# Two heads on the partitions: attention scores from two fp16 parts in a macaron block

## The chip, the cores and the metric

The kernel runs on one core of one Trainium2 chip. The metric is the device time of one execution in microseconds (us); the comparison is the median of several runs of the kernel before and of the changed one.

## What is computed

A "macaron" block over x of shape (1, 4096, 256), all in fp32: a mixture-of-experts layer with weight one half, an attention layer, and the same mixture again. Each works on a layer-normalised x and adds to x.

```python
x = x + 0.5 * ffn(layernorm(x), Wg, W1, W2, W3, Ws1, Ws2, Ws3)
x = x + attn(layernorm(x), qkv_w, qkv_b, proj_w, proj_b)
x = x + 0.5 * ffn(layernorm(x), Wg, W1, W2, W3, Ws1, Ws2, Ws3)

def attn(x, qkv_w, qkv_b, proj_w, proj_b):      # 16 heads of 16 columns
    q, k, v = split_heads(x @ qkv_w.T + qkv_b)   # each (16, 4096, 16)
    scores = q @ k.T / 4                         # (16, 4096, 4096)
    out = softmax(scores) @ v
    return merge_heads(out) @ proj_w.T + proj_b
```

The ffn routes each token to 4 of 32 experts and adds a shared expert; the change leaves it alone, but for one helper that it shares.

## The kernel before

The attention layer is written in five pieces, one after another, with a barrier of all engines between them (`attention`, L724).

**project_heads (L747)** computes the layer norm of x, Q, K and V. The weights are transposed on TensorE (PE), ScalarE (ACT) copies them out. VectorE (DVE) takes the statistics of all 32 tiles of 128 tokens in `normalise_stats`. Then a loop goes over 8 blocks of 512 tokens: DVE normalises four tiles, PE turns them, ACT copies them; PE multiplies V (L837) and DVE adds its bias into `V` in SBUF (L919); PE multiplies four tensors of 128 columns, two of Q and two of K (L854). Each of the four is split into three bf16 parts whose sum is the fp32 value: ACT writes the first part (L892) and the full value (L894) from PSUM, DVE the rest, the second and the third part (L937, L939, L941), and SP stores the three to `part_d` in DRAM (L789) out of two part buffers. ACT squares the full value (L900), PE sums the squares of each head (L846), for a bound on the scores.

**bound_shift (L951)** makes from the norms a shift for each query, so that no exponential overflows (softmax does not change with it), and a flag that says whether the bound is tight enough. **exact_shift (L1021)** runs only where the flag says no.

**attend (L1096)** is the main part. A scores matmul gives 128 keys x 512 queries. Six products of the parts (0·0, 0·1, 0·2, 1·0, 1·1, 2·0) are stacked on the partitions, 6 x 16 rows, with three rows more for the shift, 99 rows. `Q` and `K` of two heads lie in `RA` (index r); SP loads them from `part_d`, 13 transfers a head (L1144). One step k stands for 128 keys and 2048 queries of a head:
- PE: two times two scores matmuls into `psS`, three slots of 1024 columns (L1188);
- ACT: two exponentials of 128x1024 from `psS` to `probs`, a ring of four buffers (L1233);
- PE: four "weighing" matmuls (L1202), each `values` (V of the head beside ones, 32 columns) against 512 columns of `probs`, into four strips of 32 partitions of `psO`; fp32 operands run as two passes, so the trace has eight records. The ones give the sum of the probabilities.

After 32 steps (4096 keys) DVE copies `psO` out (L1255) and takes the reciprocal (L1257), and SP stores both to `head_d` (L1161). The order on each engine is written out by hand in `body`; a body holds two heads, 128 steps, and `rounds` loops it seven times and writes out the eighth. PE issues, for each k, the first half of the scores of step k+2, the weighing of step k, the second half of step k+2:

```python
def body(r2, last):
    for k in range(STEPS):
        ahead(r2, (k + 2) * CH, last)
        weigh(r2, k)
        ahead(r2, (k + 2) * CH + 1, last)
```

The semaphores: `scored` counts chunks of scores, `exped` exponentials, `pv` weighings. Scores wait for the exponential that frees their slot, a weighing for the exponentials of its step, and the first exponential of a step for the weighing two steps before (L1232).

**project_out (L1264)** multiplies by the reciprocals and the output weights, and adds to x.

## Time and profile before

| | |
|---|---|
| median of 3 runs | 3764.67 us (3762.79 to 3764.81) |
| span of the profiled execution | 3764.7 us; no other time is shown for it, and a run of 3764.67 is among the three |
| mean granted TensorE clock | 0.929 of full speed |
| PE busy (matmuls) | 3159.2 us, 84% |
| ACT busy | 2390.9 us, 64% |
| DVE busy | 921.9 us, 24% |
| POOL busy | 750.2 us, 20% |
| head projections and shift bound | 722 to 945.3 us |
| attention loops | 945.3 to 3009 us |
| output projection | 3009 to 3068 us |

How to read it: the span runs from the first to the last instruction of one profiled execution. "Busy" is time in which at least one instruction of the engine runs; matmuls are pipelined, each lasting longer than its slot, so that a PE that is always busy need not work at its peak. PE stands for matmuls and PEld for the loads of their weights. The granted clock is the share of full speed that the throttle gives TensorE. Rows name line, engine, operation, output and inputs by the program's names.

### The profile page before, as it was taken

Reading aid. Unit: us, or ns where it says so; the run is one execution under the profiler, and the core shown is the slowest. Engines: PE = TensorE matmul, PEld = TensorE weight load, DVE = VectorE, ACT = ScalarE, POOL = GpSimd, SP = SyncE. Lnnn points to the kernel's source line nnn. Section 1 sums busy time; section 2 is a strip of 40 time slices with the busy share of each in tenths; the row PEclk is TensorE's granted clock in tenths of the full one; section 3 lists DMA queues with packets and bytes.
Section 4 is the critical chain, followed back from the end, with each engine's and each line's share of the span. In section 5 each row is a group of like instructions: output and inputs, shape, how many; then the busy total and the mean of one; then the engine's idle time right before and its main releaser. Section 6 shows DMA issues by size and latency. Waiting matters only on the chain. (4 is left out here: it accounts for less than half of the span.)

```text
span 3764.7 us, 60460 instructions
## 1 busy us (share of the span) xinstructions
PE 3159.2 (84%) x16839; PEld 1226.4 (33%) x16840; DVE 921.9 (24%) x2298; ACT 2390.9 (64%) x3265; POOL 750.2 (20%) x1131
## 2 busy tenths in 40 slices
PE   4379985474999999999999999999999954799863
PEld 4156653242222222222222222222222252466532
DVE  3843334555000000000000000000000057433253
ACT  1034420043999999999999999999999900244300
POOL 0455547400000000000000000000000023555465
PEclk9999998686999999999999999999999965899987
DMA  5134443322111011011101110110110050244534
GB/s 166 58 105 131 128 111 95 120 84 69 23 21 24 4 24 21 4 24 21 23 4 24 21 22 6 24 21 4 24 21 6 4 170 13 84 132 128 121 89 123
DMA packets 143809, 216.15 MB, mean 57 GB/s; under 512 B 24992, under 2 KB 109728, under 8 KB 140448
## 3 DMA queue, kind: packets, MB, share of 16 engines
q1 hardware_dynamic: 103472, 121.24, 12.7%
q0 software_dynamic: 27648, 75.53, 7.8%
q10 hardware_dynamic: 12496, 16.78, 1.5%
q8 instruction: 124, 2.03, 0.2%
q14 instruction: 69, 0.57, 0.1%
HBM read 133.37 MB, written 80.08 MB: 57 GB/s over the span
## 5 line engine op out<-in xcount | busy, mean ns | idle before, releaser
L1233 ACT ACTIVATE probs<-psS 128x1024 f32<-128x1024 f32 x2048 | 1983.8, 1021 | 59.9 <-PE psO L1202 32.5
L1188 PE MATMUL psS<-RA 99*128 99x512 bf16 x4096 | 1072.7, 384 | 51.2 <-DMA RA<-part_d 19.1
L1202 PE MATMUL psO<-probs,values 128*32 128x512 f32 x8192 | 1097.6, 608 | 0.4 <-ACT probs L1233 0.4
L1188 PEld LDWEIGHTS psS<-RA 99*128 99x128 bf16 x4096 | 317.1, 98 | 1163.5 <-ACT probs L1233 870.3
L1255 DVE COPY sums<-psO 128x512 f32<-128x512 f32 x32 | 22.1, 692 | 1943.4 <-PE psO L1202 1943.4
L1295 POOL TENSOR_TENSOR RA<-RA,pbias 128x1024 f32<-128x1024 f32 x8 | 21.5, 2702 | 2092.2 <-DMA RA<-x_d 2092.2
L538 POOL DMA_INDIRECT xg<-xn_d,index x320 | 313.1, 978 | 264.6 <-PE psX L554 152.9
L562 PE MATMUL psH<-WE,xgt 128*128 x1280 | 355.9, 401 | 0.0
L1202 PEld LDWEIGHTS psO<-probs,values 128*32 128x32 f32 x8192 | 161.6, 108 | 439.9 <-issue 426.3
L609 ACT ACTIVATE gate<-psH 128x128 f32<-128x128 f32 x320 | 88.8, 278 | 326.2 <-PE psH L562 326.2
L669 POOL DMA_INDIRECT Y<-pair_d,cindex x256 | 246.3, 962 | 120.0 <-issue 70.5
L562 PEld LDWEIGHTS psH<-WE,xgt 128*128 128x128 f32 x1280 | 220.1, 192 | 42.6 <-issue 2.5
L577 PE MATMUL psO<-WE,hidt 128*128 x640 | 213.8, 416 | 0.2
L702 ACT ACTIVATE sgate<-psA 128x512 f32<-128x512 f32 x32 | 19.1, 597 | 306.7 <-PE psB L683 306.7
L692 PE MATMUL psZ<-ws,shid 128*128 128x256 f32 x256 | 95.4, 539 | 128.9 <-DVE shid L709 110.4
L554 PE MATMUL psX<-ident,xg 128*128 128x128 f32 x640 | 135.3, 294 | 66.9 <-DMA xg<-xn_d,index 64.3
L589 DVE COPY xgt<-psX 128x256 f32<-128x256 f32 x320 | 135.9, 425 | 148.1 <-PE psX L554 143.1
L618 ACT ACTIVATE ob<-psO 128x256 f32<-128x256 f32 x320 | 122.9, 384 | 65.7 <-PE psO L577 60.2
L594 DVE TENSOR_TENSOR hid<-gate,psH 128x128 f32<-128x128 f32 x320 | 92.1, 288 | 282.3 <-ACT gate L609 282.3
L719 DVE SCALAR_TENSOR_TENSOR RA<-Y,pair_weight,RA 128x256 f32 x256 | 124.3, 485 | 124.3 <-DMA Y<-pair_d,cindex 105.6
L609 ACT ACT_TABLE_LOAD x2 | 2.6, 1283 | 204.7 <-PEq L284 204.7
L554 PEld LDWEIGHTS psX<-ident,xg 128*128 128x128 f32 x640 | 73.1, 142 | 151.4 <-DMA xg<-xn_d,index 105.3
(191 smaller groups left out, 1980.7 us busy)
## 6 DMA issues: line engine op xcount, KB each, us to landing
pair_d<-ob SPq DMA_DIRECT2D x320, 128.0 KB, 1.8
RA<-part_d SPq DMA_DIRECT2D x192, 128.0 KB
part_d<-parts SPq DMA_DIRECT2D x32, 384.0 KB, 3.2
xn_d<-xn SPq DMA_DIRECT2D x64, 128.0 KB, 1.7
hd<-head_d SPq DMA_DIRECT2D x16, 512.0 KB, 6.7
xg<-xn_d,index POOLq DMA_INDIRECT x320, 2.8
RA<-in_x SPq DMA_DIRECT2D x8, 512.0 KB, 7.4
WE<-in_W ACTq DMA_DIRECT2D x1, 4096.0 KB, 22.9
```

Of the source, the lines that this page charges most:

```text
L538: pool.indirect_dma_start(xg[:, u, :], None, xn_d, bass.IndirectOffsetOnAxis(ap=index[:, u:u + 1], axis=0))\
L554: last = pe.transpose(psX[s % 2][:, c * P:(c + 1) * P], xg[:, (s + 2) % U, c * P:(c + 1) * P], ident[:, :])
L562: last = pe.matmul(psH[(s + 1) % 2][:, :], xgt[:, (s + 1) % 2, c * P:(c + 1) * P], WE[:, e, c * 2 * H:(c + 1) * 2 * H], start=(c == 0), st ...
L577: pe.matmul(psO[(s - 1) % 2][:, :], hidt[:, (s - 1) % 2, :], WE[:, e, DC * 2 * H:], start=True, stop=True).then_inc(sem("down"), 1)
L589: v.tensor_copy(xgt[:, s % 2, :], psX[s % 2][:, :]).then_inc(sem("xgt_ready"), 1)
L618: act.activation(ob[:, (s - 1) % U, :], psO[(s - 1) % 2][:, :], ACT.Copy).then_inc(sem("ob_ready"), 1)
L669: pool.indirect_dma_start(Y[:, s, :], None, pair_d, bass.IndirectOffsetOnAxis(ap=index[:, w, u, k:k + 1], axis=0))\
L692: last = pe.matmul(psZ[u % 2][:, :], hid[:, m, u * P:(u + 1) * P], ws2[:, m, :], start=(m == 0), stop=(m == HSC - 1))
L719: v.scalar_tensor_tensor(X[:, t, :], Y[:, (u % 2) * TOPK + k, :], pair_weight[:, bass.ds(t, 1), k], X[:, t, :], ALU.mult, ALU.add).then_in ...
L1188: last = pe.matmul(psS[slots[m]][:, b * BLK:(b + 1) * BLK], K[r][0:QROWS, kt * P:(kt + 1) * P], Q[r][0:QROWS, at:at + BLK], start=True, st ...
L1202: last = pe.matmul(psO[q % 2][32 * j:32 * (j + 1), :], values[:, r, kt, :], probs[:, m % PS, at:at + BLK], start=(kt == 0), stop=(kt == KT ...
L1233: act.activation(probs[:, m % PS, :], psS[slots[m]][:, :], ACT.Exp, scale=SCALE).then_inc(sem("exped"), 1)
```

## The change

The parts and the shapes change, from the weights on:

- **Two fp16 parts.** fp16 holds more digits than bf16 but a smaller range. `balance_weights` therefore scales the rows of the query weights and biases by powers of two and those of the keys by the inverse, before the weights are turned; it stands on DVE between the two halves of the statistics (`normalise_stats` now has two loops of four rounds, in the other layers too). ACT writes the high part, DVE the low part in one operation from PSUM. There are four part buffers, one for each of the four tensors of a block. PE waits for the split in place of ACT's second identity.
- **Two heads on the partitions.** Three products (0·0, 1·0, 0·1) take 3 x 16 rows, with three rows for the shift 51. The even head of a pair lies at partition 0, the odd one at 64. A unit is one scores matmul; successive units alternate between the heads.
- **Wider exponentials.** 128 keys x 4 units make a step. Scores go in chunks of three units (1536 columns), two slots of `psS`; 128 units of a group make 42 chunks of three and one of two. ACT does one exponential per chunk, into a ring of four buffers of 1536 columns. A body holds two pairs of heads: 8 groups, 344 chunks, 256 steps; `rounds` loops it three times and writes out the fourth.
- **Shift bound.** Two reductions over 4096 columns and the zeroing of `shift_d` go from DVE; POOL writes the ones and the step (1024) beside the keys in this piece, in eight memsets, and SP loads the operands of the first two pairs here.

```diff
-NPART = 3
-KROWS = 6 * HD
-QROWS = KROWS + NPART
+NPART = 2
+NSHIFT = 3
+SHIFT_ROW = 2 * HD
+LAST_ROW = SHIFT_ROW + NSHIFT
+ROWS = LAST_ROW + HD
+STEP0 = 1024.0
+HALF_ROWS = P // 2
...
+    for half in range(2):
+        with v.Fori(0, NT // 8) as i:
+            for u in range(4):
+                t = i * 4 + (half * (NT // 2) + u)
+                v.bn_stats(stats[:, bass.ds(t, 1), :], X[:, t, :]).then_inc(act_sem, 1)
+        if half == 0 and between is not None:
+            between()
...
+def balance_weights(v, link, raw, bias, square_sum, span, expo_i, expo_f, power, scaled):
+    HB = 2 * D // P // 2
+    link(v.tensor_tensor(span[:, :], bias[:, :], bias[:, :], ALU.mult))
+    link(v.scalar_tensor_tensor(span[:, :], square_sum[:, :], float(D), span[:, :], ALU.mult, ALU.add))
+    link(v.tensor_scalar(expo_i[:, :], span[:, :].bitcast(I32), 23, None, ALU.arith_shift_right))
+    link(v.tensor_copy(expo_f[:, :], expo_i[:, :]))
+    link(v.tensor_tensor(expo_f[:, 0:HB], expo_f[:, HB:], expo_f[:, 0:HB], ALU.subtract))
+    link(v.tensor_copy(expo_i[:, 0:HB], expo_f[:, 0:HB]))
+    link(v.tensor_scalar(expo_i[:, 0:HB], expo_i[:, 0:HB], 2, None, ALU.arith_shift_right))
+    link(v.tensor_copy(expo_f[:, 0:HB], expo_i[:, 0:HB]))
+    link(v.tensor_scalar(expo_f[:, 0:HB], expo_f[:, 0:HB], 60.0, -60.0, ALU.min, ALU.max))
+    link(v.tensor_scalar(power[:, 0:HB], expo_f[:, 0:HB], 2.0 ** 23, 127.0 * 2 ** 23, ALU.mult, ALU.add))
+    link(v.tensor_scalar(power[:, HB:], expo_f[:, 0:HB], -2.0 ** 23, 127.0 * 2 ** 23, ALU.mult, ALU.add))
+    link(v.tensor_tensor(bias[:, :], bias[:, :], power[:, :].bitcast(F32), ALU.mult))
+    for b in range(2 * HB):
+        v.tensor_scalar(raw[:, b, :], raw[:, b, :], power[:, b:b + 1].bitcast(F32), None, ALU.mult).then_inc(scaled, 1)
...
+                for n, b in enumerate((6, 7, 4, 5, 0, 1, 2, 3)):
+                    if b < NE:
+                        pe.wait_ge(sem("w_scaled"), b + 1)
+                    if n >= 2:
+                        pe.wait_ge(sem("w_out"), n - 1)
...
-                                pe.wait_ge(sem("q_out"), j * NE + (e - 1))
+                                pe.wait_ge(sem("split"), j * NE + (e - 1))
...
-                            act.wait_ge(sem(f"part_stored{e % 2}"), (j * (NE // 2) + e // 2) * 16 + 16)
-                            act.activation(parts[:, e % 2, 0, :], psQ[e % 2][:, :], ACT.Identity, bias=bias[:, e:e + 1])
+                            act.wait_ge(sem(f"part_stored{e}"), j * 16 + 16)
                             total = key_sum[:, e - 2, bass.ds(j, 1)] if e >= 2 else None
-                            act.activation(full[:, e % 2, :], psQ[e % 2][:, :], ACT.Identity, bias=bias[:, e:e + 1],
-                                           accum_out=total)\
-                               .then_inc(sem("q_out"), 1)
-                            act.wait_ge(sem("q_out"), j * NE + (e + 1))
-                            if e == 0:
-                                act.wait_ge(sem("measured"), j + 1)
-                            act.activation(square[:, e, :], full[:, e % 2, :], ACT.Square).then_inc(sem("squared"), 1)
+                            act.activation(parts[:, e, 0, :], psQ[e % 2][:, :], ACT.Identity, bias=bias[:, e:e + 1],
+                                           accum_out=total).then_inc(sem("high"), 1)
+                            if e >= 1:
+                                squared(j, e - 1)
+                            if e == NE - 1:
+                                squared(j, e)
...
+                def balance():
+                    v.wait_ge(sem("bias"), 16)
+                    v.wait_ge(sem("w_squared"), NE)
+                    balance_weights(v, own.link, raw, bias, square_sum, span, expo_i, expo_f, power, sem("w_scaled"))
+                normalise_stats(v, own.link, X, stats, mean, rstd, tmp, var, sem("stats"), sem("sqrt"), balance)
+                v.wait_ge(sem("vbias"), 16)
...
-                            n = j * NE + e
-                            f, r, g = full[:, e % 2, :], rest[:, :], parts[:, e % 2, :, :]
-                            v.wait_ge(sem("q_out"), n + 1)
-                            if not (isinstance(n, int) and n == 0):
-                                v.wait_ge(sem("split"), n)
-                            v.tensor_tensor(r, f, g[:, 0, :], ALU.subtract).then_inc(sem("rest"), 1)
-                            v.wait_ge(sem("rest"), n + 1)
-                            v.tensor_copy(g[:, 1, :], r).then_inc(sem("mid"), 1)
-                            v.wait_ge(sem("mid"), n + 1)
-                            v.tensor_tensor(g[:, 2, :], r, g[:, 1, :], ALU.subtract).then_inc(sem("split"), 1)
+                            v.wait_ge(sem("high"), j * NE + (e + 1))
+                            v.scalar_tensor_tensor(parts[:, e, 1, :], psQ[e % 2][:, :], bias[:, e:e + 1], parts[:, e, 0, :],
+                                                   ALU.add, ALU.subtract).then_inc(sem("split"), 1)
...
+            @block.gpsimd
+            def _(pool):
+                for r in range(2):
+                    for base in (0, HALF_ROWS):
+                        at = base + SHIFT_ROW
+                        pool.memset(K[r][at:at + NSHIFT, :], 1.0).then_inc(sem("ones"), 1)
+                        pool.wait_ge(sem("ones"), 4 * r + base // 32 + 1)
+                        pool.memset(K[r][at:at + 1, :], STEP0).then_inc(sem("ones"), 1)
+                        pool.wait_ge(sem("ones"), 4 * r + base // 32 + 2)
             @block.sync
             def _(sp):
-                sp.wait_ge(sem("zeroed"), 1)
-                for n in range(1, NPART):
-                    sp.dma_start(shift_d[n], zero[:, :]).then_inc(sem("shift_out"), 16)
+                for r in range(2):
+                    load_parts(sp, Q[r], K[r], part_d, r, sem(f"ops{r}"))
                 sp.wait_ge(sem("negated"), 1)
-                sp.dma_start(shift_d[0], shift[:, :]).then_inc(sem("shift_out"), 16)
-                sp.wait_ge(sem("shift_out"), 16 * NPART)
-def query_rows(sp, dst, part_d, h, signal):
-    row = 0
-    for part, times in ((0, 3), (1, 2), (2, 1)):
-        for _ in range(times):
-            sp.dma_start(dst[row:row + HD, :], part_d[part, bass.ds(h * HD, HD), :]).then_inc(signal, 16)
-            row += HD
-def key_rows(sp, dst, part_d, h, signal):
-    for n, part in enumerate((0, 1, 2, 0, 1, 0)):
-        sp.dma_start(dst[n * HD:(n + 1) * HD, :], part_d[part, bass.ds(h * HD + D, HD), :]).then_inc(signal, 16)
-def exact_shift(nc, sem, sb, pb, RA, ident, safe, part_d, shift_d):
-    ops = RA[:, :].bitcast(BF16).rearrange("p (n t) -> p n t", n=4)
+                sp.dma_start(shift_d[1], shift[:, :]).then_inc(sem("shift_out"), 16)
...
+def head_parts(sp, dst, base, part_d, first, order, signal):
+    for row, part in zip((0, HD, LAST_ROW), order):
+        sp.dma_start(dst[base + row:base + row + HD, :], part_d[part, bass.ds(first, HD), :]).then_inc(signal, 16)
+def load_parts(sp, Qr, Kr, part_d, pair, signal):
+    for n in range(2):
+        h = pair * 2 + n
+        head_parts(sp, Qr, n * HALF_ROWS, part_d, h * HD, (0, 1, 0), signal)
+        head_parts(sp, Kr, n * HALF_ROWS, part_d, h * HD + D, (0, 0, 1), signal)
+def load_shift(sp, Qr, shift_d, pair, signal):
+    for n in range(2):
+        at = n * HALF_ROWS + SHIFT_ROW
+        sp.dma_start(Qr[at:at + NSHIFT, :], shift_d[:, bass.ds(pair * 2 + n, 1), :].rearrange("a h t -> (a h) t"))\
+          .then_inc(signal, 16)
...
-    QU = T // (4 * BLK)
-    W = 2 * BLK
-    CH = 4 * BLK // W
-    STEPS = 2 * QU * KT
-    SLOTS, PS = 3, 4
...
+    QG = 4
+    GU = 4 * KT
+    WIDE = 3
+    PAIRS = NH // 2
+    RING = 4
+    GROUP = [WIDE] * (GU // WIDE) + ([GU % WIDE] if GU % WIDE else [])
+    UNITS = 2 * QG * GU
+    first, chunk_of = [], []
+    for g in range(2 * QG):
+        for size in GROUP:
+            first.append(len(chunk_of))
+            chunk_of += [len(first) - 1] * size
+    CHUNKS = len(first)
+    STEPS = UNITS // 4
+    HALF_CHUNKS = CHUNKS // 2
+    first.append(UNITS)
     CREDIT = 4
-    n_chunks = STEPS * CH
-    slots = [n % SLOTS for n in range(n_chunks)]
-    slots[-4:] = [0, 1, 2, 1]
-    LOADS = 13
-    def since(n):
-        d = 1
-        while slots[(n - d) % n_chunks] != slots[n]:
-            d += 1
-        return d
+    LOADS = 14
...
+                            sp.wait_ge(sem("scored"), r2 * CHUNKS + HALF_CHUNKS * (r + 1))
                             carried(sp, sem("seen_sp"))
-                            load(h + 2, r)
+                            load_parts(sp, Q[r], K[r], part_d, r2 * 2 + (2 + r), sem(f"ops{r}"))
...
+                def scores(r2, m, waits):
+                    if m % HALF_CHUNKS == 0:
+                        pe.wait_ge(sem(f"ops{m // HALF_CHUNKS}"), r2 * (16 * LOADS) + 16 * LOADS)
+                    if waits:
+                        pe.wait_ge(sem("exped"), r2 * CHUNKS + (m - 1))
+                    for u in range(first[m], first[m + 1]):
+                        r, q, kt, j = u // (QG * GU), u // GU % QG, u // 4 % KT, u % 4
+                        rows = slice(j % 2 * HALF_ROWS, j % 2 * HALF_ROWS + ROWS)
+                        at = (2 * q + j // 2) * BLK
+                        last = pe.matmul(psS[m % 2][:, (u - first[m]) * BLK:(u - first[m] + 1) * BLK],
+                                         K[r][rows, kt * P:(kt + 1) * P], Q[r][rows, at:at + BLK], start=True, stop=True)
...
+                        m, at = place(4 * k + j)
+                        last = pe.matmul(psO[q % 2][32 * j:32 * (j + 1), :], values[:, r, j % 2, kt, :],
+                                         probs[:, m % RING, at:at + BLK], start=(kt == 0), stop=(kt == KT - 1))
...
+                    k = 0
+                    for m in range(0, CHUNKS, 2):
+                        ahead(r2, m + 2, last)
+                        while k < STEPS and place(4 * k + 3)[0] <= m:
+                            weigh(r2, k)
+                            k += 1
+                        ahead(r2, m + 3, last)
+                    for k in range(k, STEPS):
                         weigh(r2, k)
...
-                        if m % CH == 0:
-                            act.wait_ge(sem("pv"), r2 * STEPS + (m // CH + 1))
-                        act.activation(probs[:, m % PS, :], psS[slots[m]][:, :], ACT.Exp, scale=SCALE).then_inc(sem("exped"), 1)
+                    for m in range(CHUNKS):
+                        act.wait_ge(sem("scored"), r2 * CHUNKS + (m + 1))
+                        before = m - RING
+                        done = final_step(before) + 1 if before >= 0 else final_step(CHUNKS + before) + 1 - STEPS
+                        act.wait_ge(sem("pv"), r2 * STEPS + (done + CREDIT))
+                        n = (first[m + 1] - first[m]) * BLK
+                        act.activation(probs[:, m % RING, 0:n], psS[m % 2][:, 0:n], ACT.Exp, scale=SCALE).then_inc(sem("exped"), 1)
```

**The order on PE in the loops.** L1188 and L1202 are scores and weighing before, L1256 and L1276 after; the rows named REGISTER_ALU make the value of a wait. First two steps in steady state before:

```order
L1185 REGISTER_ALU
L1188 MATMUL psS<-RA 128x512 x2
L1185 REGISTER_ALU
L1188 MATMUL psS<-RA 128x512 x2
L1202 MATMUL psO<-probs,values 32x512 x4
L1185 REGISTER_ALU
L1188 MATMUL psS<-RA 128x512 x2
```

The same place after the change, four chunks (three steps):

```order
L1276 MATMUL psO<-probs,values 32x512 x8
L1251 REGISTER_ALU
L1256 MATMUL psS<-RA 128x512 x3
L1251 REGISTER_ALU
L1256 MATMUL psS<-RA 128x512 x3
L1276 MATMUL psO<-probs,values 32x512 x4
L1251 REGISTER_ALU
L1256 MATMUL psS<-RA 128x512 x3
L1251 REGISTER_ALU
L1256 MATMUL psS<-RA 128x512 x3
L1276 MATMUL psO<-probs,values 32x512 x8
```

A weighing stood behind every four scores matmuls; now one or two of them, in turns, stand behind six, with a wait ahead of each three.

**The order on POOL ahead of the loops.** `RA` holds the operands, `values` the values and their ones. Before, in the loops' own piece:

```order
L1136 MEMSET values 128x32x16
L1138 MEMSET RA 3x4096
L1136 MEMSET values 128x32x16
L1138 MEMSET RA 3x4096
```

After, the first eight in `bound_shift`, the last in `attend`:

```order
L1048 MEMSET RA 3x4096
L1050 MEMSET RA 1x4096
L1048 MEMSET RA 3x4096
L1050 MEMSET RA 1x4096
L1048 MEMSET RA 3x4096
L1050 MEMSET RA 1x4096
L1048 MEMSET RA 3x4096
L1050 MEMSET RA 1x4096
L1015 UNCONDITIONAL_BRANCH
L1209 UNCONDITIONAL_BRANCH
L1213 MEMSET values 128x32x16 x4
```

Two memsets of 4096 columns have become eight, and they stand a piece earlier.

## Rows read from the trace of the kernel before

**Rows 1.** Windows: span part, then us, PE, PEld, DVE, ACT, POOL busy, granted clock, DMA, GB/s
```profile
722.00:945.30 223.30, 127.41 (x372) 70.17 (x373) 121.62 (x235) 77.08 (x140) 8.95 (x7) 0.74 0.32 91
...
945.30:3009.00 2063.70, 2031.17 (x12288) 478.70 (x12288) 129.33 (x76) 1992.76 (x2055) 0.00 (x0) 0.99 0.10 17
...
954.83:1200.50 245.67, 245.57 (x1500) 58.22 (x1498) 12.42 (x7) 242.25 (x250) 0.00 (x0) 1.00 0.06 11
```

**Rows 2.** Timeline, one steady step: start us, us, engine, line, operation, count
```profile
955.66 1.06 PE L1202 MATMUL psO<-probs,values 128*32 128x512 f32 x8
...
955.75 1.02 ACT L1233 ACTIVATE probs<-psS 128x1024 f32<-128x1024 f32 x1
...
956.11 0.61 PE L1202 MATMUL psO<-probs,values 128*32 128x512 f32 x4
...
956.66 0.39 PE L1188 MATMUL psS<-RA 99*128 99x512 bf16 x1
...
956.66 1.04 PE L1188 MATMUL psS<-RA 99*128 99x512 bf16 x4
...
956.79 1.03 ACT L1233 ACTIVATE probs<-psS 128x1024 f32<-128x1024 f32 x1
...
957.63 1.06 PE L1202 MATMUL psO<-probs,values 128*32 128x512 f32 x8
```

**Rows 3.** Timeline of the loops: the first step, and two later rounds' first exponentials
```profile
947.73 3.77 ACT L1233 ACTIVATE probs<-psS 128x1024 f32<-128x1024 f32 x4
...
948.80 0.13 PEld L1188 LDWEIGHTS psS<-RA 99*128 99x128 bf16 x2 [1.68 <-ACT probs L1233]
...
1203.44 3.77 ACT L1233 ACTIVATE probs<-psS 128x1024 f32<-128x1024 f32 x4
...
1462.22 3.77 ACT L1233 ACTIVATE probs<-psS 128x1024 f32<-128x1024 f32 x4
```

**Rows 4.** Groups by line: count, busy us, mean ns, idle before and releasers
```profile
L1233 ACT ACTIVATE probs<-psS 128x1024 f32<-128x1024 f32 x2048 | 1983.8, 1021 | 59.9 <-PE psO L1202 32.5
...
L609 ACT ACTIVATE gate<-psH 128x128 f32<-128x128 f32 x320 | 88.8, 278 | 326.2 <-PE psH L562 326.2
...
L941 DVE TENSOR_TENSOR parts<-rest,parts 128x512 bf16<-128x512 f32 x32 | 22.2, 692 | 1.1
...
L1138 POOL MEMSET RA<- 3x4096 bf16 x2 | 7.2, 3588 | 0.1
```

**Rows 5.** Timeline of two blocks of the head projections
```profile
832.62 0.69 ACT L892 ACTIVATE parts<-psQ,bias 128x512 bf16<-128x512 f32 x1 [8.93 <-PE psQ L854]
...
839.29 0.69 ACT L892 ACTIVATE parts<-psQ,bias 128x512 bf16<-128x512 f32 x1 [1.87 <-DMA part_d<-parts]
...
844.93 3.78 PE L837 MATMUL psV<-wt,axnt 128*128 128x256 f32 x8 [4.69 <-DVE RB L919]
...
852.59 0.69 ACT L892 ACTIVATE parts<-psQ,bias 128x512 bf16<-128x512 f32 x1 [9.33 <-PE psQ L854]
```

**Rows 6.** Timeline of the start of the head projections
```profile
725.69 10.32 SPq L781 DMA_DIRECT2D bias<-in_qkv_b  x1
...
725.99 9.95 DVE L189 BATCH_NORM_STATS2 astats<-RA  x28 [0.36 <-issue]
...
742.32 1.38 DVE L924 TENSOR_SCALAR axn<-RA,amean,arstd 128x256 f32<-128x256 f32 x4 [3.62 <-DMA vbias<-in_qkv_b]
...
746.00 6.45 PE L837 MATMUL psV<-wt,axnt 128*128 128x256 f32 x16 [1.24 <-ACT axnt L883]
```

**Rows 7.** Timeline of the shift bound and the first scores
```profile
908.01 0.14 DVE L948 COPY key_mean<-psN 16x1 f32<-16x1 f32 x1 [0.29 <-PE psN L865]
...
909.65 1.76 DVE L971 MEMSET zero_shift<- 16x2048 uint32 x1 [1.49 <-PEq L775]
...
930.79 2.73 SPq L1012 DMA_DIRECT2D RA<-part_d  x6
...
945.29 2.74 PE L1188 MATMUL psS<-RA 99*128 99x512 bf16 x6 [19.05 <-DMA RA<-part_d]
```

270 lines of the change are left out of this document (136 added, 134 removed).

## The prediction

> **What bounds the kernel now.** I read the windows first. Of 3764.7 us, 2063.7 go to the attention loops and 223.3 to the head projections and the shift bound ahead of them [rows 1]; both feed-forward layers lie outside the change, but for one helper. In the loops PE is busy 98%, ACT 97%, so neither share says who waits. The timeline of one steady step does. PE starts the second pass of a weighing (fp32, four strips) at 956.11, four scores matmuls at 956.66 and the next weighing at 957.63, with no hole beyond about 0.1 us at each switch: the 0.55 from 956.11 to 956.66 is 0.43 of streaming plus 0.12, and four scores at 0.22 each (1.04 less the last one's 0.39, by three) leave 0.09 of the 0.97 [rows 2]. On ACT the exponential at 956.79 starts 1.04 after that at 955.75, though an exponential that waits for nothing follows its forerunner by 0.92 (four take 3.77: 3.77 less 1.02, by three) [rows 2, 3]. It starts 1.13 after the weighing at 955.66 began, each time: it waits for the ring of probabilities. So **PE sets the pace**, one step of 4 x 512 columns in 1.965 us (250 exponentials, two a step, in 245.67 [rows 1]), and ACT has 0.12 us a step to spare.
>
> **Loops, part 1: what each instruction costs after.** An activation of 128 columns takes 278 ns and one of 1024 takes 1021 [rows 4]: 0.83 ns a column and 0.17 us fixed. Of 1536 columns one takes 1.45; waiting for nothing it follows its forerunner by 0.92 + 0.43 = 1.35. The weighings keep form and number (0.45 + 0.43, and the switch). The scores shrink from 99 rows to 51. That alone I cost at nothing: a matmul's time is that of its 512 columns. But two heads now lie at rows 0 and 64, and successive matmuls alternate. The trace has no row-packed pair. The nearest row is the weighing: four matmuls on disjoint column strips, in two passes, take 1.06 together against 0.61 for one pass [rows 2]. Bounds for the pair: 0.22 (together) and 0.44 (one after the other). I take 0.22, because the strips that exist do overlap. Three scores matmuls then take two slots, 0.43, instead of 0.65. The Trainium skill (TensorE: Matmul & The Clock Gate, Part 3: Packing small matmuls) gives 3.07 times for four row tiles, not 4; were a pair as inefficient, my estimate by that page is 0.28 for it, and the sum below would be 15 us higher. No row here can show that.
>
> **Loops, part 2: the order, which is what counts.** The rows of the order show it: after the scores of chunk m+2 (they wait for exponential m) come one or two weighings, then the scores of m+3. With four part buffers of probabilities, exponential m+2 may start only when chunk m-2 has been weighed out, and in every second group that is the first weighing *behind* the scores of m+2. So there is a cycle from exponential m to m+2:
> - exponential m starts; scores that wait for its end start 1.07 later at 1024 columns (947.73 to 948.80 [rows 3]), so 1.07 + 0.43 = 1.50 at 1536;
> - three scores until the weighing begins: 0.97 less two of the four slots of 0.22 = 0.54;
> - weighing begins until the exponential that waits for it: 955.66 to 956.79 = 1.13 [rows 2].
>
> Together 3.17 for two chunks, where ACT alone would need 2 x 1.35 = 2.70. A group is 128 units: 42 chunks of three and one of two, 43 in all, so groups start alternately on even and odd chunks. Even start: 21 pairs x 3.17 and 0.6 for the short one, partly under the last hole: 67.2. Odd start: the cycle binds only in every second pair (for the other the weighing is already done). A binding pair costs 3.17, the other 2.70, and 0.08 more where scores stand behind two weighings: 5.95 for four chunks, 63.5 a group. Eight of each: 8 x 67.2 + 8 x 63.5 = **1046 for half the heads, 2091 in all**, against 2048 exponentials x 0.983 = 2012.5 now: **+79**.
>
> **Loops, part 3: turn-arounds.** The loop body comes round in 258.8 us (1203.44 to 1462.22 [rows 3]), of which 256 x 0.983 = 251.6 are the pace: 7.2 here, and 7.6 on the mean of five such rounds: table load, cold PE, "issue". Six such ends now (eight rounds, the last written out), two afterwards (four rounds, bodies of 344 exponentials): **-30**. An operand load of a later pair starts when its scores are issued, a half body (250 us) ahead; its 14 transfers are covered.
>
> **Head projections.** A block of 512 tokens takes 19.97 (832.62 to 852.59 [rows 5]); 19.9 on the mean of the eight between 746.00 and 908.01 [rows 6, 7], with 2.8 of tail. In it PE needs at full clock, by the slots of rows 2: V 16 x 0.22 = 3.5, queries and keys 16 x 0.44 = 7.0, turning about 1.0, norms 4 x 0.22 = 0.9: 12.4. The rest is waiting: ACT's first identity waits 1.87 for a store out of the two part buffers; PE waits 4.69 for V's additions, which stand behind DVE's three splitting operations, and then takes 3.78 for eight V matmuls, which are 8 x 0.22 at full clock [rows 5]. After: four part buffers, no second identity on ACT, one DVE operation for three (0.69, as L941 [rows 4]; were it a fused one's double, V's additions still come within a slot), and a third reduction of norms under PE. PE now releases a psQ buffer only at the split; that falls under the next tensor. I take 13.3 a block (12.4 and about 0.9 for switches and the loops' branches): 8 x 6.6 = **-53**; bounds 16 a block (-31) and 12.6 (-58).
>
> **Before them.** The weights' balancing stands on DVE between the halves of the statistics and waits for the bias. That load now precedes the copy of x; its issue alone takes 10.32 from 725.69 [rows 6], and a landing of some 2.5 gives 738. Then 12 chained small ones (0.2 each) and four of about 0.4: 742; half of the statistics (9.95 for 28 of 32 [rows 6]: 5.7) and the moments (2.5): xn at 751 against 742.32 [rows 6]: **+9**, bounds +4 and +12. The helper's second loop costs the two other layers about 1 us each: **+2**.
>
> **Shift bound and start.** DVE loses two reductions of 4.4 and a memset, but POOL gains eight memsets one behind another in the same block, where the nearest row has 3588 ns for 3 x 4096 [rows 4]: 28.6 (a block begins 1.6 after 908.01, at 909.65). From there to the first load of operands, 930.79, are 21.1 [rows 7]; DVE's last result comes 4.2 ahead of that, barriers and the check of the flag, and these stay. The loads of the first two pairs go under the memsets; behind the barrier only the shift rows are left, two issues of 0.3 and a landing of about 3, where now 14.5 pass from 930.79 to 945.29 [rows 7]. So 1.6 + 28.6 + 4.2 + 3.7 = 38.1 after 908.01, against 37.3: **+1**. If one row costs a third of three, -9.
>
> **Sum.** +79 - 30 - 53 + 9 + 2 + 1 = +8. The profiled execution has 3764.7 us of span and no time around it that is shown; the median of the runs is 3764.67, so the sum starts from either. That gives 3773; taking back 2 for slots rounded up (0.215 as 0.22), I state **3771**. Differences under 0.2% (7.5 us) no measurement here tells from none.
>
> **Rivals.**
> 1. *The row pair does not overlap* (slower; the change would not do what the stacking says). For it: in the trace all scores matmuls follow each other at 0.22, and no row-packed pair exists. Against: column strips overlap. Price: 0.22 more in each cycle, 3.39 for a pair, and in odd groups 0.22 more at the scores behind two weighings too (5.95 + 2 x 0.22 = 6.39 for four chunks): 21 x 3.39 + 0.6 = 71.8 and 68.1, eight of each 1119, 2238 in all, +147; less 3 for the short ones: **3915**. It decides early: 252 binding pairs, so a row pair that takes 0.25 in place of 0.22 costs 8 already. Chance 0.13. The Trainium skill (TensorEngine Tiling, PSUM pressure) says that row tiles may not write one PSUM bank together; here each unit has its own bank, so this is no reason for it.
> 2. *The ring does not bind* (faster): the first weighing is out before ACT asks. For it: ACT's wait of 0.12 today is small, and the order of the wait is read from instructions, not seen for this shape. Then only scores behind two weighings delay ACT: ready 1.50 + 0.54 + 2 x 0.90 + 0.10 + 0.60 = 4.54 after exponential m, where ACT wants them after 3 x 1.35 = 4.05. Four chunks take 5.9: 344 x 5.9 less 32 x 0.43 = 2016, -75: **3696**. Were ACT alone the bound, 1344 x 1.35 + 32 x 0.92 = 1844 would give 3524 (-247), but a pair of weighings (1.8) and two switches do not fit under one exponential. Chance 0.12, the latter 0.02 of it.
> 3. *The clock falls* (slower): PE would stand still about a quarter of each cycle, where it is granted 1.00 now [rows 1]; in the projections at 57% busy it was 0.74. At 1.2 GHz streaming takes twice the time, as V's eight matmuls show (3.78 for 1.76 [rows 5]): the cycle's 0.54 and the weighing's 0.90 double, 1.4 more in 3.17, and 2091 x 0.44 = +920: near 4690. Against: no hole would be over 0.6 us. Chance 0.05.
>
> **How the numbers follow.** The forecast's case has 0.70. Its terms move by 21 (the cycle, 1% of 2091), 22 (blocks) and 5 (start), seldom together: 3735 to 3810. Of it 0.28 lies below 3757, 0.26 within 0.2%, 0.46 above 3772. Faster: 0.20 + 0.12 = 0.32; same 0.18; slower 0.32 + 0.13 + 0.05 = 0.50. For 8 in 10 the range must take in the non-overlapping pair at 3915, and below the forecast's own low end part of the way to rival 2: 3715 to 3920.
>
> **What would show it.** Right: exponentials 1.45 long, their starts in turns 1.35, 1.82 / 1.42, 1.74; ACT waiting for psO; pairs of scores matmuls starting within 0.01; blocks of 13 us; memsets of 28 us under the first loads; two turn-arounds. Wrong: ACT without holes (rival 2), scores at 0.22 each (rival 1), a clock under 1.00 in the loops (rival 3). The weakest step is the cycle: if starts two chunks apart differ by 2.9 or less, this forecast fails.

## The result, and the profile after

| | before | changed |
|---|---|---|
| median | 3764.74 us (3762.79 to 3765.47, 4 runs) | 6375.73 us (6375.38 to 6376.65, 4 runs) |
| ratio | 1 | 1.6935 (95% interval 1.6911 to 1.6959) |
| span of the profiled execution | 3764.7 | 6374.0 |
| mean granted clock | 0.929 | 0.758 |

The prediction said 3771, with a range of 3715 to 3920. It was wrong by 2605 us. The page of the changed kernel shows where they lie: the rows of section 2 (each digit a fortieth of the span, 159 us) and the costliest groups.

```profile
span 6374.0 us, 74864 instructions
...
PE   3797667777777777777777888888888888865984
...
DVE  5433558888888888888889000000000000036334
ACT  1241210000000000000000999999899988931420
...
PEclk9998765555555555555555999999999999976997
...
L1147 DVE TENSOR_REDUCE half_max<-psSx 128x2048 f32 x1024 | 2297.6, 2285 | 275.9 <-PE psSx L1127 242.6
L1127 PE MATMUL psSx<-exact_ops 51*128 51x512 f16 x4096 | 1913.8, 620 | 666.2 <-DVE half_max L1147 417.0
L1305 ACT ACTIVATE probs<-psS 128x1536 f32<-128x1536 f32 (+1 forms) x1376 | 1913.8, 1441 | 188.7 <-PE psO L1276 184.5
L1256 PE MATMUL psS<-RA 51*128 51x512 f16 x4096 | 824.2, 385 | 360.5 <-ACT probs L1305 351.7
```

From the seventh slice to the twenty-second ACT does nothing, DVE is busy and the granted clock is 0.5. The two groups at the head, L1147 and L1127, are in `exact_shift`, which reads every score once (1024 maxima over 2048 columns, 2.28 us each) to find the shift of each query. The trace of before has no such group: there the branch was not taken. The timeline of the changed kernel gives the piece its borders:

```profile
854.06 0.15 DVE L1000 COPY key_mean<-psN 16x1 f32<-16x1 f32 x1 [0.29 <-PE psN L910]
...
863.37 0.14 DVE L1029 TENSOR_SCALAR safe<-worst 1x1 int32<-1x1 f32 x1
...
899.05 1.46 PE L1127 MATMUL psSx<-exact_ops 51*128 51x512 f16 x3 [35.92 <-DMA exact_ops<-part_d]
...
1198.01 9.10 DVE L1147 TENSOR_REDUCE half_max<-psSx 128x2048 f32 x4 [0.17 <-PE psSx L1127]
...
3502.50 1.46 PE L1256 MATMUL psS<-RA 51*128 51x512 f16 x6 [6.53 <-POOL values L1213]
```

The flag is written at 863.37, and the first scores of the loops start at 3502.50, 2648 after `key_mean`, where [rows 7] has 37.3. Outside that stretch the kernel's time is near what was forecast. The windows (columns as in [rows 1]) show three stretches: the head projections and the bound up to the end of the memsets, the exact pass, and the loops. Behind them stands the steady state of the loops.

```profile
721.80:884.10 162.30, 109.07 (x371) 61.25 (x371) 82.22 (x190) 58.45 (x117) 30.01 (x12) 0.82 0.41 107
884.10:3502.50 2618.40, 1920.18 (x4112) 434.99 (x4113) 2327.16 (x1126) 0.00 (x0) 2.75 (x4) 0.50 0.03 5
3502.50:5614.00 2111.50, 1757.13 (x12288) 347.94 (x12288) 129.17 (x75) 1917.60 (x1379) 0.00 (x0) 0.99 0.05 9
```

```profile
3519.17 2.89 ACT L1305 ACTIVATE probs<-psS 128x1536 f32<-128x1536 f32 x2 [0.38 <-PE psO L1276]
3522.34 2.79 ACT L1305 ACTIVATE probs<-psS 128x1536 f32<-128x1536 f32 x2 [0.28 <-PE psO L1276]
3525.51 2.89 ACT L1305 ACTIVATE probs<-psS 128x1536 f32<-128x1536 f32 x2 [0.38 <-PE psO L1276]
...
3575.59 5.58 ACT L1305 ACTIVATE probs<-psS 128x1536 f32<-128x1536 f32 x4 [0.38 <-PE psO L1276]
3581.54 5.58 ACT L1305 ACTIVATE probs<-psS 128x1536 f32<-128x1536 f32 x4 [0.38 <-PE psO L1276]
```

Two exponentials every 3.17 us in a group that starts on an even chunk, four every 5.95 in one that starts on an odd chunk, each time behind a hole that `psO` (the weighing) ends. These are the two numbers of the forecast's cycle.

### The profile page after: what moved, and what is told of

Its sections match the earlier page's. It is cut to its first block and busy times, and to the rows that moved or that the text cites. A ratio compares the mean times of both kernels' runs of the same rounds, so it can differ in the third digit from the quotient of the medians.

```text
span 6374.0 us, 74864 instructions
## 1 busy us (share of the span) xinstructions
PE 4789.0 (75%) x20949; PEld 1523.3 (24%) x20952; DVE 3209.2 (50%) x3378; ACT 2297.0 (36%) x2566; POOL 774.0 (12%) x1140
## 5 line engine op out<-in xcount | busy, mean ns | idle before, releaser
L1147 DVE TENSOR_REDUCE half_max<-psSx 128x2048 f32 x1024 | 2297.6, 2285 | 275.9 <-PE psSx L1127 242.6
L1127 PE MATMUL psSx<-exact_ops 51*128 51x512 f16 x4096 | 1913.8, 620 | 666.2 <-DVE half_max L1147 417.0
L1305 ACT ACTIVATE probs<-psS 128x1536 f32<-128x1536 f32 (+1 forms) x1376 | 1913.8, 1441 | 188.7 <-PE psO L1276 184.5
L1256 PE MATMUL psS<-RA 51*128 51x512 f16 x4096 | 824.2, 385 | 360.5 <-ACT probs L1305 351.7
L1276 PE MATMUL psO<-probs,values 128*32 128x512 f32 x8192 | 1025.9, 603 | 0.5 <-ACT probs L1305 0.5
L1127 PEld LDWEIGHTS psSx<-exact_ops 51*128 x4096 | 433.3, 125 | 2136.7 <-issue 2136.7
L1256 PEld LDWEIGHTS psS<-RA 51*128 51x128 f16 x4096 | 151.8, 93 | 1275.3 <-ACT probs L1305 983.4
L1276 PEld LDWEIGHTS psO<-probs,values 128*32 128x32 f32 x8192 | 196.2, 109 | 494.2 <-issue 484.0
```

The lines of the kernel that those rows point to most:

```text
L1127: last = pe.matmul(psS[n][:, b * BLK:(b + 1) * BLK], ops[0:ROWS, 0, bass.ds(t * P, P)], ops[0:ROWS, 1, n * HALF + b * BLK:n * HALF + (b + ...
L1147: v.tensor_reduce(half[:, bass.ds(t, 1), n], psS[n][:, :], AX, ALU.max).then_inc(sem("x_read"), 1)
L1256: last = pe.matmul(psS[m % 2][:, (u - first[m]) * BLK:(u - first[m] + 1) * BLK], K[r][rows, kt * P:(kt + 1) * P], Q[r][rows, at:at + BLK], ...
L1276: last = pe.matmul(psO[q % 2][32 * j:32 * (j + 1), :], values[:, r, j % 2, kt, :], probs[:, m % RING, at:at + BLK], start=(kt == 0), stop= ...
L1305: act.activation(probs[:, m % RING, 0:n], psS[m % 2][:, 0:n], ACT.Exp, scale=SCALE).then_inc(sem("exped"), 1)
```

## The experiments

The chips that these runs were on differ in time by 0.7%, so each was timed beside the kernel before on its own chip, and runs of different chips are compared by their ratios to it.

### The branch: rounding, and the limit of the flag

Why should the flag fall, when the scores are the same? `balance_weights` takes for each of 256 pairs of rows (a query's and its key's) the difference of two exponents, shifts it right by two and scales one side up and the other down. An arithmetic shift rounds towards minus infinity: 0 to 3 give 0, but -1 gives -1. By a working of mine from the inputs (not read from a run), 67 of the 256 differences are -1 and none is beyond 1; their queries are halved, their keys doubled. Products stay the same, but the bound multiplies the norm of the longest query of a head by that of its longest key (and of its mean key), and the doubled rows of one then meet the rows of the other that weren't halved: 284.5 by that working, against 167.4 without scaling, and the flag allows 280 (SAFE, which is 70, divided by the scale of a quarter). Theory A: the rounding sets off the branch, and without it the forecast stands.

`e1_round` adds 2 before the shift, so that the quarter is rounded to the nearest (-1 to 0):

```diff
-    link(v.tensor_copy(expo_i[:, 0:HB], expo_f[:, 0:HB]))
+    link(v.tensor_scalar(expo_i[:, 0:HB], expo_f[:, 0:HB], 2.0, None, ALU.add))
```

> Edit: in the balancing of the weights 2 is added before the exponent difference is shifted right by two, so that a difference of -1 gives 0 as +1 does, not -1; nothing else. Theory A (the floor of the shift moves a factor of two from some query rows to key rows, that blows up the bound on the scores, and the flag sends the kernel into exact_shift): the branch is gone, 3502.5 us (first scores in the changed kernel) less 892 (854.06 + 0.6 + 29.4 of memsets + 4.2 + 3.5) = 2610 fall away, 3765 us, DVE without L1147. Theory B (the flag is false for another reason: the fp16 shift, the new bound from query_norm, or a value that is no number): unchanged at 6376. In the loops both expect what the changed kernel shows: exponentials two chunks apart by 3.17.

Measured: 3764.61 us (3761.98 to 3767.27, 11 runs), ratio 0.9993 (0.9984 to 1.0002). One DVE operation on 128x2 numbers stands between 6376 and 3765. That needn't yet be the bound; two runs of the changed kernel as it is, with another limit, ask for its value:

```diff
-SAFE = 70.0
+SAFE = 71.0     # e2_limit284; 71.25 in e3_limit285
```

> Edit: the changed kernel with SAFE = 71, so LIMIT = 284 in place of 280. Theory A puts the bound only little above 280: a factor of two on the rows that are shifted at most doubles a bound that passed 280 before; my own estimate from the inputs' norms is 284.5, so 284 still takes the branch: 6376. Theory B (a bound far off or no number): 6376 too. The pair with the next run tells them apart.

> Edit: the changed kernel with SAFE = 71.25, so LIMIT = 285. Theory A: the bound lies between 284 and 285, the branch is not taken, 3765. Theory B: 6376.

Measured, one run each: 6376.91 us with a limit of 284, 3763.73 with 285. So the bound lies between the two, 1.4 to 1.8% above the limit of 280, and theory A is shown. The second run is the changed kernel word for word but for the limit, so the branch costs 6375.73 - 3763.73 = 2612 us. Does the branch cost so much because of the new parts? `e6_before_safe41` puts the limit of the old kernel at 164:

```diff
-SAFE = 70.0
+SAFE = 41.0
```

> The kernel before, with SAFE 41 instead of 70: the flag's limit falls from 280 to 164. By my working of the bound from the inputs (about 167 in the old kernel, where no weights are balanced) the flag then says no, and the old kernel runs its own exact_shift too. Theory 'the 2612 us is the price of the branch, not of the new parts': near 3765 + 2600 = 6370, up to 6500 as its operands are 96 rows of bf16; DVE's reductions of 2048 columns take the same 2.2 to 2.6 us each. Theory 'the branch is slow only with fp16 or 51 rows': well under 5000. If my bound is wrong and under 164: 3765.

Measured: 6415.32 us (one run), beside 3792.88 of the kernel before on that chip, 2622 more. The group of maxima costs what it costs in the changed kernel:

```profile
L1062 PE MATMUL psSx<-RA 96*128 96x512 bf16 x4096 | 1928.5, 627 | 644.3 <-DVE half_max L1080 351.1
L1080 DVE TENSOR_REDUCE half_max<-psSx 128x2048 f32 x1024 | 2287.4, 2286 | 303.7 <-PE psSx L1062 303.7
```

It also shows that the old kernel's bound lies between 164 and its limit of 280, so at most a factor of 1.7 below it: doubling the longest keys of a head could be enough.

### The loops: whether the row pair overlaps, and who makes ACT wait

With the branch out of the way `e1_round` is the forecast's kernel, and the further edits start from it. Rival 1 had the scores of two heads, at rows 0 and 64, run one after another. `e7_one_row_tile` puts both at rows 0 to 50; it is there for its time alone and leaves out the odd head's scores:

```diff
-                        rows = slice(j % 2 * HALF_ROWS, j % 2 * HALF_ROWS + ROWS)
+                        rows = slice(0, ROWS)
```

> e1_round with the odd head's scores taken from rows 0 to 50 too, so that no two successive scores matmuls lie on disjoint rows. It leaves out the odd head's scores (the even head's stand in their place); number, shape and order of instructions stay. This puts a price on rival 1. Theory 'the row pair overlaps and the cycle of 3.17 us counts it once': three scores take three slots of 0.22 instead of two, +0.22 in each cycle, 2238 instead of 2091 in the loops: 3764.6 + 147 = about 3910 (3890 to 3925), a binding pair of exponentials 3.39 apart by its starts. Theory 'overlap is worth nothing, successive scores hide under something else': 3765, pairs still 3.17 apart.

Measured: 3935.75 us (4 runs), ratio 1.0377 (1.0362 to 1.0393), on a chip where before takes 3792.88; times 3767.24, which before took beside `e1_round`, this is 3909. PE and ACT of that kernel, and PE of the changed one:

```profile
1101.48 0.82 PE L1256 MATMUL psS<-RA 51*128 51x512 f16 x3
...
1101.62 2.79 ACT L1305 ACTIVATE probs<-psS 128x1536 f32<-128x1536 f32 x2 [0.28 <-PE psO L1276]
1105.00 1.45 ACT L1305 ACTIVATE probs<-psS 128x1536 f32<-128x1536 f32 x1 [0.59 <-PE psO L1276]
...
1108.39 2.79 ACT L1305 ACTIVATE probs<-psS 128x1536 f32<-128x1536 f32 x2 [0.28 <-PE psO L1276]
```

```profile
3519.89 0.60 PE L1256 MATMUL psS<-RA 51*128 51x512 f16 x3
...
3521.21 1.06 PE L1276 MATMUL psO<-probs,values 128*32 128x512 f32 x8
```

Three scores matmuls take 0.60 on alternating rows and 0.82 on the same rows: the pair costs one slot of 0.22, and the binding cycles went from 3.17 to 3.39 (1101.62 to 1105.00 to 1108.39). Rival 1 falls, and the price that it was given, 147, is near the 144 measured (3909 less 3764.6).

The other question is the ring. The forecast held that exponential m+2 waits for a weighing that stands behind the scores of m+2. `e4_order` lets PE issue each weighing as soon as its last chunk is through:

```diff
-                    for m in range(0, CHUNKS, 2):
+                    for m in range(CHUNKS):
                         ahead(r2, m + 2, last)
                         while k < STEPS and place(4 * k + 3)[0] <= m:
                             weigh(r2, k)
                             k += 1
-                        ahead(r2, m + 3, last)
```

> Edit: e1_round, and PE's order in the loops: after the scores of chunk m+2 come the weighings whose last chunk is at most m, for every m, in place of one or two of them behind every second chunk. Theory C (in the changed kernel the ring of four binds: the weighing that frees exponential m+2's buffer is queued behind scores that wait for exponential m; 3.17 a pair): now each weighing is out before ACT asks, PE needs per four chunks 4 x 0.43 + 3 x 0.90 + 6 x 0.09 = 5.0 and ACT 4 x 1.35 = 5.4, so ACT is the bound: 1344 x 1.35 + 32 x 0.92 = 1844 for 2087, 3765 - 240 = 3525. Theory D (the hole of ACT comes from the switches of PE's tiling, not from the ring): there are twice as many switches here, so it gets slower, by 344 x 2 x 0.19 = 130 at most, or stays.

Measured: 3522.95 us (3518.64 to 3525.7, 5 runs), ratio 0.9354 (0.9341 to 0.9366). ACT hardly waits any more:

```profile
1099.73 25.82 ACT L1304 ACTIVATE probs<-psS 128x1536 f32<-128x1536 f32 x19
```

```profile
L1304 ACT ACTIVATE probs<-psS 128x1536 f32<-128x1536 f32 (+1 forms) x1376 | 1851.9, 1451 | 11.2 <-PE psS L1256 6.5 <-issue 0.8
```

Nineteen exponentials in 25.82, 1.35 apart, and 11.2 us of waiting ahead of all 1376, where the changed kernel has 188.7: ACT is the bound now. The same finer order with each weighing one chunk later (`<= m - 1` in place of `<= m`), `e9_order_late`, separates "the ring" from "finer turns":

> e1_round with the order of e4_order, but each weighing one chunk of scores later (the weighings whose last chunk is m-1 or less stand behind the scores of chunk m+2). The ring of four stays. Theory 'the ring makes a cycle: an exponential waits for the weighing of four chunks before, and that stands behind scores': the wait binds in more pairs than in the original order; my count of the cycle gives 2150 in the loops against 2087, +63: about 3828 (3800 to 3860). Theory 'e4_order gained from issuing three scores at a time instead of six (finer turns), the ring does not matter': as e4_order, about 3523. Theory 'order does not matter much, e4 gained by chance of alignment': near 3765.

Measured: 3860.55 us (4 runs), ratio 1.0178 (1.0163 to 1.0194), or 3834 at the before of `e1_round`. That is +70 where +63 was counted. With the same scores, weighings and exponentials the two kernels differ by 0.0824 of the time of before (1.0178 less 0.9354), 310 us, by their order alone: the place of the weighing is what counts. In its trace nearly every pair has its hole, in odd groups too:

```profile
1099.38 2.98 ACT L1304 ACTIVATE probs<-psS 128x1536 f32<-128x1536 f32 x2 [0.38 <-PE psO L1276]
1102.55 2.79 ACT L1304 ACTIVATE probs<-psS 128x1536 f32<-128x1536 f32 x2 [0.19 <-PE psO L1276]
```

A ring of three or five buffers wasn't tried: a body has 344 chunks, of which neither is a divisor, so a buffer's number would change from round to round.

### The head projections: ring or work

`e10_two_parts` is `e1_round` with two part buffers. The stores and their counts follow, and ACT also waits for its square of the tensor two before, which reads the same buffer:

```diff
-        parts = sb("parts", [P, NE, NPART, BLK], F16, c)
+        parts = sb("parts", [P, 2, NPART, BLK], F16, c)
...
-                            act.wait_ge(sem(f"part_stored{e}"), j * 16 + 16)
+                            act.wait_ge(sem(f"part_stored{e % 2}"), (j * (NE // 2) + e // 2) * 16 + 16)
```

> e1_round with two part buffers in the head projections, as the kernel before has, in place of four; ACT's identity of one tensor waits until the tensor two before is stored. This asks which of the two edits made the block of 512 tokens shorter (19.9 to 13.3 by my count, 13.4 measured): the larger ring, or the two operations fewer on DVE and one fewer on ACT. Theory 'work': V's additions no longer stand behind three splits, and a store of 256 KB lands within two tensors (2 x 1.72 us); the store wait returns at most 0.6 a block, so 3765 + 0 to 5. Theory 'ring': the wait of 1.87 in each block for a store comes back, once or twice a block: 8 x 1.87 x 1 to 2 = +15 to +30: 3780 to 3795.

Measured: 3790.03 us (11 runs), ratio 0.9992 (0.9983 to 1.0001), as `e1_round`. From the first `axn` to `key_mean` pass 114.4 us, against 113.2 in `e1_round`. The wait is there, once a block, and a third as long as the 1.87 of [rows 5]:

```profile
810.18 0.69 ACT L949 ACTIVATE parts<-psQ,bias 128x512 f16<-128x512 f32 x1 [0.63 <-DMA part_d<-parts]
```

So the larger ring gave 1.2 of the 53 us that these blocks lost, and the rest came with the work taken out (and the shorter stores, 256 KB for 384). The trace of the changed kernel shows where, beside the 4.69 and 3.78 of [rows 5]:

```profile
786.50 1.99 PE L882 MATMUL psV<-wt,axnt 128*128 128x256 f32 x8 [0.36 <-DVE RB L977]
...
791.50 0.69 ACT L947 ACTIVATE parts<-psQ,bias 128x512 f16<-128x512 f32 x1 [5.13 <-PE psQ L899]
...
804.47 0.69 ACT L947 ACTIVATE parts<-psQ,bias 128x512 f16<-128x512 f32 x1 [5.12 <-PE psQ L899]
```

PE waits 0.36 for V's additions in place of 4.69, and its eight V matmuls then take 1.99 in place of 3.78: 6.1 of the 6.9 us by which a block is shorter (12.97, 791.50 to 804.47). The second of these two is the clock, 0.50 from 844.93 to 848.70 before and 1.00 from 760 to 790 after. From the first `axnt` to `key_mean` the same 346 matmuls kept PE busy for 120.8 us at a granted clock of 0.82 before, and for 102.5 us at 0.96 after. Which of the operations taken out matters most, those of DVE or that of ACT, wasn't tried.

### The shift bound: three attempts at 15 us

The eight memsets of POOL took 29.4 us on the way to the loops (854.69 to 884.1), so dividing or halving them should pay. All three build on `e4_order`. `e8_order_memsets` gives four of them to DVE:

```diff
+                for r in range(2):
+                    at = HALF_ROWS + SHIFT_ROW
+                    own.link(v.memset(K[r][at:at + NSHIFT, :], 1.0))
+                    own.link(v.memset(K[r][at:at + 1, :], STEP0))
```

> e4_order with the eight memsets of the key rows divided: four on POOL as before, four on DVE behind the flag. Theory 'the memsets are on the path of the shift bound': POOL's four take 14.7 us instead of 29.4, DVE's four (1.8 each, by the memset of 2048 columns of 32 bits) end about 12 us after the block's start, so the first scores come 13 to 14 us earlier: 3523 - 13 = 3510 (3505 to 3515). Theory 'something else in that piece (the loads of 11 us and their landings) ends last': 3518 to 3523.

Measured: 3550.32 us (5 runs), ratio 0.9363 (0.935 to 0.9376), no gain beside the 0.9354 of `e4_order`. In its trace the first scores come 31.9 us after `key_mean`, 2.9 sooner, and not 13 to 14. DVE took 3.47 for one, not 1.8, and began after the flag, so its last memset ended at 897.67, 27.0 after `key_mean`:

```profile
881.05 3.47 DVE L1032 MEMSET RA<- 3x4096 f16 x1 [0.91 <-DVE safe L1029]
```

The 1.76 of [rows 7] was for 2048 words of 32 bits, and the price went by elements. `e11_order_memset32` writes two fp16 as one word:

```diff
-                        pool.memset(K[r][at:at + NSHIFT, :], 1.0).then_inc(sem("ones"), 1)
+                        pool.memset(K[r][at:at + NSHIFT, :].bitcast(I32), 0x3C003C00).then_inc(sem("ones"), 1)
```

> e4_order with the eight memsets of the key rows written as 32-bit words (two fp16 in each, 2048 elements a row instead of 4096), all on POOL. e8_order_memsets showed that DVE's memset of 4096 fp16 takes 3.47 us, as long as POOL's 3.50, while DVE's of 2048 words of 32 bits takes 1.76 in the kernel before. Theory 'a memset costs by the element, on both engines': 1.75 each, 14.3 for eight instead of 29.4, and then the shift's own chain ends last (its store issued 11 us after the block's start): first scores 15 us earlier, ratio 0.9354 - 0.0040 = 0.931. Theory 'POOL's cost goes by bytes': no change, ratio 0.935 to 0.936. Theory 'POOL's cost is mostly fixed or depends on the type otherwise': in between.

Measured: 3546.75 us (5 runs), ratio 0.935 (0.9337 to 0.9363), again no gain clear of the interval, though seven of the eight memsets now take 1.80. From `key_mean` to the first scores pass 32.1 us (34.8 in `e4_order`). The waits of SP's queue name what ends next:

```profile
SPq L1015 <- DMA shift_d<-shift: 15.2, 1, 15.2
```

The store of the shift, 128 KB, stands on its queue behind 24 operand loads of 128 KB. `e12_late_pair` moves the twelve of the second pair behind it, into the loops' piece:

```diff
-                for r in range(2):
-                    load_parts(sp, Q[r], K[r], part_d, r, sem(f"ops{r}"))
+                load_parts(sp, Q[0], K[0], part_d, 0, sem("ops0"))
                 sp.wait_ge(sem("negated"), 1)
...
+                load_parts(sp, Q[1], K[1], part_d, 1, sem("ops1"))
```

> e11_order_memset32 with the loads of the second pair of heads moved from the shift bound into the loops' own piece, behind the shift rows of the first pair. In e11 the memsets took 1.80 each and were over 16.4 us after key_mean, but the first scores came only 32.1 after it (34.8 before); SP waited 15.2 us there for the store of the shift, which stands behind 24 loads of 128 KB on its queue. Theory 'the store of the shift waits in the queue behind the loads': with 12 of the 24 loads ahead of it, it lands before the memsets end (12 loads take about 12.5 us at the 130 GB/s of e11), the next piece starts about 18 us after key_mean, the first scores about 21 to 22 after it: 10 us less than e11, ratio 0.9350 - 0.0027 = 0.932 to 0.933. Theory 'the store itself takes that long': first scores still 32 after key_mean, ratio 0.935. Theory 'the first scores wait for operands next': somewhere between 22 and 32.

Measured: **3510.0 us** (3507.57 to 3511.58, 5 runs), ratio 0.9319 (0.9307 to 0.9332), against 3765.8 of the kernel before; the interval lies clear of that of `e11_order_memset32`. The timeline of `e12_late_pair`:

```profile
856.03 0.15 DVE L1000 COPY key_mean<-psN 16x1 f32<-16x1 f32 x1 [0.29 <-PE psN L910]
...
863.28 0.33 SPq L1057 DMA_DIRECT2D shift_d<-shift  x1
...
870.62 1.80 POOL L1050 MEMSET RA<- 1x2048 int32 x1
...
877.31 1.46 PE L1256 MATMUL psS<-RA 51*128 51x512 f16 x6 [13.76 <-DMA RA<-shift_d]
```

The first scores come 21.3 us after `key_mean`, 13.5 sooner than in `e4_order`, and SP's wait for the store of the shift is 7.7. The memsets had hidden the queue; whether the loads alone, moved with the memsets left at 3.50, bring anything wasn't run (POOL's own 29.4 us argue against it). This is the fastest version found.

## Why the prediction was wrong, and where it was right

**The step that failed** is in "Shift bound and start": "barriers and the check of the flag, and these stay". It put a price on reading the flag and none on what the flag decides. What it put at nothing took 2612 us: the change of the weights lifted the bound to between 284 and 285, over the limit of 280, and the exact pass ran. No rival had it, and the range could not hold it: the largest, the fallen clock, ended near 4690. The trace of before could not show the danger, since a branch that isn't taken leaves no row, and the size of the bound is in none. The diff and the inputs could: a scaling of weights ahead of a bound made of norms, a shift that rounds -1 to -1, and norms that a numerical working from the inputs puts over the limit (284.5 by mine, done after the result). "Before them" costs that very chain on DVE to a fifth of a microsecond an operation, but never asks what its numbers do.

The other steps can be read in `e1_round`, where only the branch is missing (3764.61, forecast 3771), and in the changed kernel's own trace outside the branch:

- **Loops, parts 1 to 3** (+79 and -30, so +49). From the first exponential to the last copy of `sums` pass 3009.15 - 947.73 = 2061.4 before and 5614.2 - 3504.9 = 2109.3 in the changed kernel: +47.9. In its first rounds even and odd groups take 66.8 and 64.1 (forecast 67.2 and 63.5, the same sum within 0.2), so parts 1 and 2 came as they were worked out. The two ends of a looped round that are left take 4.8 and 3.8, forecast 7.6. Cycle (3.17, 5.95), exponential (1.45) and slot of the pair (0.22) came as forecast, by the rows above, and `e4_order`, `e9_order_late` and `e7_one_row_tile` show the mechanism by taking it away, worsening it and pricing it. By the Trainium skill's figure for four row tiles (TensorE: Matmul & The Clock Gate, Part 3: Packing small matmuls) the prediction's estimate for a pair was 0.28; 0.60 against 0.82 for three matmuls doesn't bear that out for two row tiles. Its price for a slower pair was too low: the 252 binding pairs are those of half the heads. With 504 a pair of 0.25 costs at least 15, not 8, and one of 0.28 at least 30, not 15; the sum of rival 1, with +147 for 0.22 more, gives 40 for 0.06.
- **Head projections** (-53). First V matmul to `key_mean`: 162.0 before (746.00 to 908.01), 109.1 after (744.98 to 854.06): -52.9. The block takes 12.97, forecast 13.3; V's additions no longer hold PE up, as forecast.
- **Before them** (+9) was wrong in kind. From the piece's first issue to `axn` pass 18.4 before (723.88 to 742.32) and 19.6 after (721.82 to 741.37): +1.1. The 10.32 of the load of `bias` [rows 6] was not its own. It was the first issue behind the copy of x; in the changed kernel the load stands ahead of that copy and takes 0.37, and of the two issues behind the copy, the zeroing of the shift, which take 11.41 together, nobody waits for either. So balancing begins at 729.78, not 738. It adds 4.7 to DVE's chain, but the 3.62 for which `axn` waited for `vbias` before [rows 6] are gone, since that load no longer stands behind the copy either:

```profile
723.18 0.37 SPq L817 DMA_DIRECT2D bias<-in_qkv_b  x1
...
724.62 11.41 SPq L823 DMA_DIRECT2D shift_d<-zero_shift  x2
```

- **Shift bound and start** (+1, without the branch). Memsets 29.4 (28.6 forecast), `key_mean` to first scores 34.8 in `e1_round` (857.09 to 891.92), 38.1 forecast and 37.3 before: -2.5.
- **The helper's second loop** (+2) can't be told from noise: behind the last copy of `sums` pass 755.5 before, and between 754.0 (`e4_order`) and 760.1 (`e12_late_pair`) in the kernels that follow.
- **Rivals.** 1 fell (`e7_one_row_tile`). 2 fell for this order, and its second branch, ACT alone the bound at 3524, is what `e4_order` reached by the order (3522.95): the forecast's remark that two weighings don't fit under one exponential holds, but issuing one at a time they needn't. 3 fell: the loops are granted 0.99 with PE busy 83% (1757 of 2111.5); the 0.50 lies in the exact pass and about the first 10 us of the loops.

For `e1_round` the forecast's "no difference" holds, and mostly by its mechanism: the loops are 48 us slower and the projections 53 us faster, as worked out. The +9 rested on a misread row; that the number hardly suffered is due to its size and not to the working. As a forecast of the changed kernel it missed what mattered.

## What to carry to other kernels

Where a kernel branches on its data, a change ahead of the branch is costed with the values, not the instructions: work the tested quantity out from the inputs, compare it with its limit, and give the other side of the branch a chance and a price (here DVE's 1024 maxima over 2048 columns could have been priced from the trace of before, at half the 4.4 us of a reduction over 4096: about 2250 us, where 2298 were measured). A ring's wait is a matter of order: read on the other engine what stands ahead of the instruction that frees the buffer. A DMA's long issue may tell of the queue, not of the transfer: here, after a reordering, another one paid; and what a shortened stretch brings is bounded by what ends second in it.

## What was not expected of the hardware

- A memset's time went by the elements of a partition, whatever their size (two bytes or four) and whether on one partition or three, on both engines. On POOL 3x4096 and 1x4096 fp16 took 3.50 us each, 3x2048 and 1x2048 words of 32 bits 1.80; on DVE 3.47 and 1.76 for the same two lengths. The forecast's bound "if one row costs a third of three" had no ground. The Trainium skill (VectorE: DVE Perf Modes, Zero memsets can be issued as uint32) says that a memset's time goes by elements whatever the type, and recommends wider words for zeros on the Vector engine. DVE's rows agree (3.47 and 1.76); here it also held on POOL and for 1 and 1024.
- POOL's memsets and one operation of DVE, the negation of the shift, shut each other out. The negation took 3.81 on DVE beside fp16 memsets, 2.26 beside memsets of words. In the changed kernel the memset that began at 858.25 ended at 861.75; the negation ended 1.08 later, at 862.83, and the next memset took 0.97 longer than the others:

```profile
858.25 3.50 POOL L1050 MEMSET RA<- 1x4096 f16 x1
...
859.02 3.81 DVE L1024 TENSOR_SCALAR shift<-shift 16x4096 f16<-16x4096 f16 x1 [3.77 <-ACT shift L1034]
...
861.81 4.47 POOL L1048 MEMSET RA<- 3x4096 f16 x1
```

  In `e11_order_memset32` the same sum holds: memset over at 875.96, negation at 877.04, next memset 2.77 for 1.80. By the Trainium skill (SBUF — State Buffer, Who interferes with whom) a `tensor_scalar` can run in a two-port mode, and then it and a GpSimd instruction exclude each other for their whole length; both traces agree, and the negation's own time is then about 1.1 us. The trace of before bears that out, where POOL does nothing beside the same operation (in bf16):

```profile
924.78 1.22 DVE L980 TENSOR_SCALAR shift<-shift 16x4096 bf16<-16x4096 bf16 x1
```

- In the exact pass the granted clock was 0.50, the lower of its two levels (1.2 of 2.4 GHz), for 2600 us, with PE busy 73% of them (1920 of 2618). It was 0.50 before the pass too: from 855 to 898 PE had worked 0.18 us. It rose between 3512 and 3516, 10 us into the loops, when PE had been busy 5.0 of the 6 us before. Why it stayed low through the pass no run shows. DVE, busy 89%, was the bound, so a full clock could have given back at most the 276 us for which DVE waited ahead of its maxima.
